# Moving a head's factor from VectorE's row maximum to ScalarE's exponential

## The reference

```
qkv     = x @ w_qkv.T                       # 16 heads, q, k and v of 128 each
logits  = q @ k.T / sqrt(128)               # 1024 x 1024 for each head
weights = softmax(logits)                   # over the keys
out     = (weights @ v) @ w_out.T
```

## Time and profile before

| | |
|---|---|
| median of 3 runs | 882.39 us (881.47 to 882.75) |
| profiled execution | 882.52 us, of which its span is 880.7 us |
| TensorE / VectorE / ScalarE / GpSimd busy | 93% / 87% / 69% / 49% of the span |
| mean granted TensorE clock | 0.99 |

### The profile page before, as it was taken

The page is one execution under the profiler, slowest core; times in us unless marked ns, Lnnn a source line. Parts: engine busy times, 40 slices in busy tenths (PEclk is TensorE's granted clock), DMA queues, the critical chain, the costliest instruction groups (busy, mean ns, idle before and its releaser), DMA issues.

```text
span 880.7 us, 13310 instructions
## 1 busy us (share of the span) xinstructions
PE 815.8 (93%) x4386; PEld 474.4 (54%) x4386; DVE 770.5 (87%) x1726; ACT 604.2 (69%) x1044; POOL 430.1 (49%) x459
## 2 busy tenths in 40 slices
PE   7889989999999989998998999989988999998997
PEld 3445544455455445454445454567755566564687
DVE  4888999999999999999999999856789898986646
ACT  5777767776778676776766776765765777768632
POOL 3334454444454448678769776125333454544300
PEclk8999999999999999999999999999989999999999
DMA  3588859957788668776875676821000000000001
GB/s 105 123 180 157 151 113 173 194 113 153 166 166 155 127 130 151 148 143 117 161 149 111 124 142 130 155 79 46 1 1 1 1 1 1 1 1 2 1 1 49
DMA packets 276869, 86.32 MB, mean 98 GB/s; under 512 B 267584, under 2 KB 272448, under 8 KB 276416
## 3 DMA queue, kind: packets, MB, share of 16 engines
q1 hardware_dynamic: 275520, 80.05, 47.0%
q0 software_dynamic: 992, 5.34, 2.2%
q10 hardware_dynamic: 288, 0.07, 0.0%
HBM read 17.29 MB, written 1.05 MB: 21 GB/s over the span
## 4 chain that ended last, share of the span: by engine, by line
DVE 41%; PE 38%; issue 9%; ACT 6%; DMA 3%; POOL 2%; DVEq 0%; SPq 0%; ACTq 0%; POOLq 0%
DVE EP L1689 11%; DVE ps L1674 10%; PE ps L1012 6%; PE ps L1014 5%; PE ps L1013 5%; PE ps L1035 4%; DVE ptm L1790 4%; PE ps L1246 3%; PE ps L1050 3%; PE ps L1281 3%; PE ps L1267 3%; DMA ET<-EP 2%; DVE OL L1750 2%; DVE ps L1873 2%; DVE rinv L1684 1%
## 5 line engine op out<-in xcount | busy, mean ns | idle before, releaser
L1445 ACT ACTIVATE EP<-ps,rinv 128x1024 f16<-128x1024 f32 x128 | 142.5, 1113 | 47.5 <-DVE rinv L1684 45.4
L1435 ACT ACTIVATE ps<-ps,nmax 128x1024 f32<-128x1024 f32 x128 | 139.3, 1088 | 49.2 <-DVE nmax L1674 42.8
L1674 DVE CUSTOM_DVE_ANT_0 ps<-ps,zero,q_unit 128x1024 f32<-128x1024 f32 x128 | 163.6, 1278 | 1.6 <-PE ps L1014 1.6
L1689 DVE SCALAR_TENSOR_TENSOR EP<-ps,rinv,EP 128x1024 f16<-128x1024 f32 x128 | 163.4, 1277 | 0.8 <-ACT EP L1445 0.5
L2039 POOL TENSOR_TENSOR wgu<-wgu,ptm 128x688 f32<-128x688 f32 x60 | 99.1, 1651 | 45.3 <-DVE ptm L1790 43.4
L1012 PE MATMUL ps<-ET,VH 128*128 128x512 f16 x256 | 97.0, 379 | 9.5 <-DMA ET<-EP 5.0
L1012 PE MATMUL ps<-K,Q 128*128 128x512 f16 x256 | 97.5, 381 | 8.7 <-DVE KR L1654 4.5
L2039 POOL TENSOR_TENSOR wdn<-wdn,ptm 128x512 f32<-128x512 f32 x45 | 57.2, 1272 | 93.2 <-DVE ptm L1790 92.1
L1014 PE MATMUL ps<-K,QR 128*128 128x512 f16 x256 | 97.0, 379 | 0.0
L1013 PE MATMUL ps<-KR,Q 128*128 128x512 f16 x256 | 97.0, 379 | 0.0
L1014 PE MATMUL ps<-ET,VL 128*128 128x512 f16 x256 | 97.0, 379 | 0.0
(11 more groups left out here) (256 smaller groups left out, 2119.3 us busy)
## 6 DMA issues: line engine op xcount, KB each, us to landing
wqr<-in_wqk SPq DMA_DIRECT2D x16, 256.0 KB, 3.6
wgu<-in_tern POOLq DMA_DIRECT2D x3, 1024.0 KB, 6.6
wvr<-in_wv SPq DMA_DIRECT2D x8, 256.0 KB, 4.1
wor<-in_wo SPq DMA_DIRECT2D x16, 128.0 KB, 3.1
ET<-EP SPq DMA_TRANSPOSE x128, 4.3
X<-in_x SPq DMA_DIRECT2D x2, 512.0 KB, 5.7
prw<-in_down_idx POOLq DMA_DIRECT2D x2, 256.0 KB, 5.1
tern<-in_l_wuq_rep SPq DMA_DIRECT2D x1, 512.0 KB, 4.1
```

Of the source, the lines that this page charges most:

```text
L1435: e.activation(bank, bank, ACT.Exp, bias=nmax[:, c:c + 1], scale=-1.0, accum_out=rsum[:, c:c + 1]).then_inc(exped.sem, 1)
L1445: e.mul(EP[:, n % NE_RING, 0, :], SB(u, j), rinv[:, c:c + 1]).then_inc(e_hi.sem, 1)
L1674: e.tensor_tensor_reduce(SB(u, j), SB(u, j), zero[:, :].broadcast_to([P, 1024]), UNIT(h), 3.0e38, ALU.add, ALU.min, nmax[:, c:c + 1]).then ...
L1689: e.scalar_tensor_tensor(out=EP[:, n % NE_RING, 1, :], in0=SB(u, j), scalar=rinv[:, c:c + 1], in1=EP[:, n % NE_RING, 0, :], op0=ALU.mult, ...
```

## The change

The row maximum becomes a plain reduction over the raw scores, negated, into a new tile `nraw`; it writes nothing back over the scores. ScalarE multiplies it with the head's factor, which is now positive, into `nmax`, waits on a semaphore of its own (`shifted`) for that product, and takes the exponential of the raw scores with the factor as its per-row scale and `nmax` as its bias. The wait for the factor (`q_back`) moves from VectorE to ScalarE, GpSimd's wait before it writes the factor anew is for the exponential instead of the maximum, and a memset of a one-column tile at the start falls away.

```diff
--- before.py
+++ after.py
@@ -313,7 +313,6 @@
         wdn = sbuf(top, "wdn", [P, 6, D])
         lut = sbuf(top, "lut", [P, 16])
         filler = sbuf(top, "filler", [P, 512], BF16)
-        zero = sbuf(top, "zero", [P, 1])
 
         with ExitStack() as ctx:
             VH, VL = (sbuf(ctx, n, [P, 2, NT, 256], F16) for n in ("VH", "VL"))
@@ -336,6 +335,7 @@
             OH, OL = (sbuf(ctx, n, [P, 4, 512], F32R) for n in ("OH", "OL"))
             rsc = sbuf(ctx, "rsc", [P, 8])
             nmax = sbuf(ctx, "nmax", [P, 8])
+            nraw = sbuf(ctx, "nraw", [P, 8])
             rsum = sbuf(ctx, "rsum", [P, 8])
             rinv = sbuf(ctx, "rinv", [P, 8])
             prw = sbuf(ctx, "prw", [P, NI])
@@ -445,6 +445,7 @@
         v_norm, v_power, v_factor, v_unit = (signal(n, "DVE") for n in ("v_norm", "v_power", "v_factor", "v_unit"))
         qkv_hi, exped, e_hi, o_hi = (signal(n, "ACT") for n in ("qkv_hi", "exped", "e_hi", "o_hi"))
         qkv_lo, maxed, e_lo, o_lo, inverted = (signal(n, "DVE") for n in ("qkv_lo", "maxed", "e_lo", "o_lo", "inverted"))
+        shifted = signal("shifted", "ACT")
         o_added, sum_down = signal("o_added", "DVE"), signal("sum_down", "DVE")
 
         abs_summed, all_summed = signal("abs_summed", "ACT"), signal("all_summed", "PE")
@@ -560,7 +561,6 @@
 
         half_set.mark(0)
         filler_set.mark(0)
-        filler_set.mark(1)
         ones_in.mark(0)
         for t in range(2):
             index_in[t].mark(t)
@@ -604,6 +604,7 @@
             elif what == "max":
                 maxed.mark(*at)
             elif what == "exp":
+                shifted.mark(*at)
                 exped.mark(*at)
             elif what == "row_inv":
                 sum_down.mark(*at)
@@ -1432,7 +1433,11 @@
                     if u >= 2:
                         w.wait_ge(*inverted[u - 2, j])
                     bank = SB(u, j)
-                    e.activation(bank, bank, ACT.Exp, bias=nmax[:, c:c + 1], scale=-1.0,
+                    h = unit(u)[0]
+                    w.wait_ge(*q_back[h])
+                    e.mul(nmax[:, c:c + 1], nraw[:, c:c + 1], UNIT(h)).then_inc(shifted.sem, 1)
+                    w.wait_ge(*shifted[u, j])
+                    e.activation(bank, bank, ACT.Exp, bias=nmax[:, c:c + 1], scale=UNIT(h),
                                  accum_out=rsum[:, c:c + 1]).then_inc(exped.sem, 1)
                 elif what == "cast_e":
                     u, j = at
@@ -1668,11 +1673,8 @@
                     w.wait_ge(*scored[u, j])
                     if u >= 2:
                         w.wait_ge(*exped[u - 2, j])
-                    h = unit(u)[0]
-                    w.wait_ge(*q_back[h])
-                    w.wait_ge(*filler_set[1])
-                    e.tensor_tensor_reduce(SB(u, j), SB(u, j), zero[:, :].broadcast_to([P, 1024]), UNIT(h), 3.0e38,
-                                           ALU.add, ALU.min, nmax[:, c:c + 1]).then_inc(maxed.sem, 1)
+                    e.tensor_reduce(nraw[:, c:c + 1], SB(u, j), AX.X, ALU.max,
+                                    negate=True).then_inc(maxed.sem, 1)
                 elif what == "row_inv":
                     u, j = at
                     c = 4 * (u % 2) + j
@@ -1955,7 +1957,6 @@
                     e.memset(f32(KT[i][rows, hh, :]), 0.0).then_inc(zeroed.sem, 1)
 
             e.memset(filler[:, :], 1.0).then_inc(filler_set.sem, 1)
-            e.memset(zero[:, :], 0.0).then_inc(filler_set.sem, 1)
             e.memset(mhalf[:, :], -0.5).then_inc(half_set.sem, 1)
             e.memset(f32(ones[:, :]), 1.0).then_inc(ones_in.sem, 1)
             for step in HEADS:
@@ -1978,10 +1979,10 @@
                     o, i0, i1 = 2 * (h0 // 2 % 2) + h0 % 2, 2 * (h0 % 2), 2 * (h0 % 2 + n)
                     for h in range(h0 - 4, h0 - 4 + n):
                         if h >= 0:
-                            w.wait_ge(*maxed[unit_of(h, 1), 3])
+                            w.wait_ge(*exped[unit_of(h, 1), 3])
                     if h0 >= 2:
                         w.wait_ge(*q_back[h0 - 1])
-                    e.tensor_scalar(q_part[:, i0 // 2:i1 // 2], wpow[:, i0:i1:2], -SCALE0 * 2.0 ** 106, None,
+                    e.tensor_scalar(q_part[:, i0 // 2:i1 // 2], wpow[:, i0:i1:2], SCALE0 * 2.0 ** 106, None,
                                     ALU.mult).then_inc(q_part_set.sem, 1)
                     w.wait_ge(*q_part_set[h0])
                     e.tensor_tensor(q_unit[:, o:o + n], q_part[:, i0 // 2:i1 // 2], wpow[:, i0 + 1:i1:2],
```

## The result

The changed kernel takes 885.5 us (median of 10 runs) against 882.5 us for the kernel before (median of 10): ratio 1.0033, 95% interval 1.0019 to 1.0047, or +2.9 us (1.7 to 4.1). It is slower, as forecast; the forecast of +6.0 us was about twice too large. Ratios are taken without two stray executions, one of 2066 us (e7) and one of 1630 us (the kernel before beside e9).

The account below looks back on a forecast made before the run. VectorE and TensorE, nearly full in the heads' stage, were taken as the bound. Net delays before `row_inv` of +3.8 us, plus 1.5 and 2.0, less 1.3, made +6.0 on 882.5 us: 888.4 us, range 878 to 897.

Parts of the forecast that it names:

- The bound and the mechanism: Heads' stage: VectorE and TensorE nearly full; anything between maximum and exponential is pure latency on a chain returning as `row_inv`.
- some 8 us: Predicted VectorE waiting before `row_inv` in all, grown from almost nothing.
- Part 1, the maximum: VectorE's plain reduction instead of the fused form: held 1.14 us instead of 1.20, saving 7.5 us at most.
- The rival that rested on no saving: VectorE's reduction held 1.20 us as before, so no place gains: count +11.4 us, 896 us in all; chance 0.13.
- Part 2 and 3: ScalarE, each tile: added product with its wait, 0.32 us; exponential's scale as per-row operand, +0.082 us.
- The count of margins: 128 pairs, row sum written to `row_inv`: lateness beyond each pair's spare time costs 8.6 us, gains 4.8, net +3.8.
- What lies behind it on ScalarE: ScalarE work queued behind product and exponential, 0.40 us longer per tile, delays VectorE: +1.5, +2.0 and -1.3 us.
- +1.5 us for OL: VectorE's attention-product wait OL, late by up to 0.3 us in five units because ScalarE reaches f0 late.
- +2.0 for `rest_e`: Some ten places where `rest_e` starts as soon as `cast_e`, late from a busy ScalarE, ends: 2 us, estimated.
- less 1.3: VectorE waits that come from TensorE take in delays lying before them: 1.3 us off.
- The GpSimd wait that moved: GpSimd's wait before rewriting the factor, now for the exponential: costed at nothing, with 38 us of cover.
- the forecast's own range: Times for the favoured case, slower by +2 to +10 us: 884.5 to 893 us; chance 0.57.

Follow-up runs that it names:

- e7: Kernel before with table-entry slot p1 moved ahead of `row_inv` of tile 0, only in iterations 17 to 29 without 26: 880.39 against 883.05 us.
- e9: Changed kernel with the 128x1 product on VectorE, right behind the reduction, instead of on ScalarE: 901.2 us against 883.17 for the kernel before.
- e1: Changed kernel without ScalarE's product and its wait, the exponential's bias a zero column: 878.09 us against 882.61 for the kernel before.
- e2: Changed kernel with a second product, by a column of ones, also waited for: 903.6 us against 882.61 for the kernel before.
- e3: Kernel before with one ScalarE product more, waited for, VectorE's fused instruction kept: 890.55 against 882.61 us.
- e4: Kernel before with the exponential's scale of -1 read from a column instead of an immediate: 883.79 against 882.61 us.
- e8: Changed kernel with slot p1 moved ahead of `row_inv` of tile 0, only in iterations 17 to 29 without 26: 882.96 us against 883.05 for the kernel before.

## Why the prediction was right or wrong

**The bound and the mechanism: right.** A product between maximum and exponential is latency on a chain that ends in VectorE's `row_inv`, and there it showed: idle time before it 2.8 to 12.5 us. I had said "some 8 us", and it is 9.7 more. e1 shows that the product decides the sign, and e2 that the price rises as margins are used up.

**Part 1, the maximum.** Duration 1209 ns against 1219 and 1215 worked out. The term was 128 x 0.059 us; measured from start to next start it is 0.069 us, 8.8 us instead of 7.5. VectorE's busy time fell by 6.9 us only, since its other instructions took some 2 us more between them in this profile. The Trainium skill (page "VectorE: DVE Perf Modes", section "Rules for kernel authors") calls the reduction the slowest VectorE operation. Here it was not: at 1209 ns it was 69 ns shorter than the form that it replaced (1278 ns) and shorter than `rest_e` over as many elements (1277 ns in the earlier trace rows). The rival that rested on no saving is excluded.

**Part 2 and 3.** Product 294 ns against 285, its wait 0.033 against 0.035, exponential +89 ns (1177 against 1088) against +82. The row sum landed 0.29 us later, forecast 0.3.

**The count of margins: the method held, with inputs on the dear side.** It took the row sum 0.307 us later, where 0.291 was measured, and VectorE 0.058 us sooner, where 0.069 was. +3.8 us forecast; +2.2 with the measured pieces; +2.9 measured. In the other runs it gave +19.9 for e2 (measured +20.5), +9.5 for e3 (+7.3), +2.0 for e4 (+0.6) and -8.1 for e1 (-4.9). For e9 it gave +17 with the price expected and 23 with the price found (+18.8). So it was off by 0.6 to 2.2 us in e2, e3 and e4, 3.2 us too far in e1 and 4 us too high in e9. That +2.2 and +2.9 lie so close is therefore in part luck.

**The step that failed** is "What lies behind it on ScalarE": +1.5 us for OL and +2.0 for `rest_e`, less 1.3, were estimates with a count and no pairing of rows. In the profile after, OL waits 5.8 us in the stage, at 15 places (6.3 before, at 10), and `rest_e`'s waiting for `cast_e` is 1.1 us in all (0.5 before, in the earlier trace rows the idle ended by EP). Both together are about nil, and so is the sum of all VectorE's waits other than that before `row_inv`, 20.8 us before and 20.7 after. ScalarE took 45 us more work in its idle time, and behind the exponential VectorE lost nothing by it that shows. So the net +2.2 us measured nothing. Without it the forecast would have been +3.8 us, inside the measured 1.7 to 4.1. It had been put on top of a count that already held the main delays. A second, smaller part of the miss is in the count itself: its inputs made +3.8 of what the measured pieces make +2.2.

**The rest.** The GpSimd wait that moved, the lacking memset and the moved wait for the factor show no cost in the groups after (neither profile shows idle time of GpSimd before `q_part`); no experiment took them alone. The range held the time; the forecast's own range of 884.5 to 893 did too.

## What to carry to other kernels

An operation moved from a full engine to an idle one is not free if it lands between a result and its waiter. Pair each result with its use over all tiles, write down the margins, and charge only what exceeds them; the sum over places was good to some 2 us in 880 here in four of six kernels, and off by 3 to 4 us in the other two (e1 and e9). And do not add guessed follow-up terms to such a count: pair the rows for them too, or leave them out. Here the small step between two large ones was cheapest as an operand of one of them. And where an experiment gives the time that was forecast, look whether the wait that it was made for has shrunk: in e7 and e8 it had hardly done so.

## What had not been expected of the hardware

A short dependent instruction on VectorE costs more than the time that it holds the engine. In e9 the 128x1 product with a per-row scalar had a mean of 214 ns and held VectorE 0.13 us (307.38 to 307.51). But it started 0.04 us after the end of the reduction (306.13 + 1.21 = 307.34 against 307.38), where an instruction that does not need the reduction's result starts 0.07 to 0.08 us before that end (423.59 against 422.45 + 1.21 = 423.66). So the step costs VectorE 0.25 us in all (1.38 - 1.13 in the medians). On ScalarE the same product took 0.33 us from its start to that of the exponential (423.70 to 424.03).
